# An attention walk over edges: one-hots written in 32 bits by VectorE without the widening copy, and a maximum moved ahead of collecting and one-hot

## The reference, cut to what matters

```
feat  = (h @ W).reshape(N, H, D)
e     = leaky_relu(el[src] + er[dst], 0.2)
emax  = segment_max(e, dst);  ex = exp(e - emax[dst])
denom = segment_sum(ex, dst)
rst   = segment_sum(feat[src] * (ex / denom[dst])[..., None], dst)
```

## Time and profile before

| | us |
|---|---|
| median of 3 runs | 6529.58 |
| lowest, highest | 6528.3, 12715.31 |
| profiled execution, its own time | 6532.67 |
| its span, first to last instruction | 6530.9 |

### The profile page before, as it was taken

The page is one execution under the profiler, slowest core; times in us unless marked ns, Lnnn a source line. Parts: engine busy times, 40 slices in busy tenths (PEclk is TensorE's granted clock), DMA queues, the critical chain, the costliest instruction groups (busy, mean ns, idle before and its releaser), DMA issues. The chain is left out here.

```text
span 6530.9 us, 127122 instructions
## 1 busy us (share of the span) xinstructions
PE 5098.4 (78%) x34156; PEld 4113.7 (63%) x34157; DVE 3381.7 (52%) x10342; ACT 2222.7 (34%) x6042; POOL 2219.6 (34%) x2057
## 2 busy tenths in 40 slices
PE   2665655428888888884797899999899997299997
PEld 1443332215555555554796688887788886299997
DVE  6898766528888888887455421113411114422222
ACT  0345666615555555556232300001200002433332
POOL 2577777765555555552221000000000000612221
PEclk8898777669999999995898999999999997599998
DMA  4478888875555555554565244442222223466665
GB/s 134 129 234 273 278 287 289 290 196 146 146 147 146 146 148 146 146 147 129 163 179 163 79 162 162 152 161 100 72 98 93 94 98 118 133 187 181 181 182 165
DMA packets 504762, 1057.75 MB, mean 162 GB/s; under 512 B 59670, under 2 KB 370317, under 8 KB 484972
## 3 DMA queue, kind: packets, MB, share of 16 engines
q1 hardware_dynamic: 385276, 706.86, 34.2%
q0 software_dynamic: 112144, 268.88, 15.0%
q10 hardware_dynamic: 7200, 80.28, 3.1%
HBM read 741.74 MB, written 323.21 MB: 163 GB/s over the span
## 5 line engine op out<-in xcount | busy, mean ns | idle before, releaser
L690 POOL DMA_INDIRECT arena<-table,arena x1664 | 1738.4, 1045 | 980.3 <-DVE arena L795 584.7
L1303 PE MATMUL banks<-arena 128*128 128x256 bf16 x14700 | 1623.7, 273 | 24.7 <-DMA arena<-counts 24.7
L1303 PEld LDWEIGHTS banks<-arena 128*128 128x128 f16 x14700 | 1439.5, 98 | 205.0 <-DMA arena<-counts 25.5
L869 PE MATMUL banks<-arena 128*128 128x261 f32 x3328 | 1009.5, 428 | 192.2 <-DVE arena L807 125.1
L620 PE MATMUL banks<-arena 128*128 128x392 bf16 x2368 | 602.2, 408 | 414.2 <-ACT banks L648 226.5
L2026 POOL DMA_INDIRECT expert_in<-arena,slot x147 | 161.2, 1097 | 2158.1 <-DVEq L1971 2116.4
L869 PEld LDWEIGHTS banks<-arena 128*128 128x128 f32 x3328 | 596.7, 199 | 330.5 <-DVE arena L807 134.0
L620 PEld LDWEIGHTS banks<-arena 128*128 128x128 bf16 x2368 | 338.2, 149 | 677.7 <-issue 635.4
L1357 DVE TENSOR_TENSOR rings<-rings,banks 128x256 f32<-128x256 f32 x98 | 41.3, 422 | 1344.1 <-PE banks L1295 1344.1
L2209 ACT ACTIVATE rings<-banks,b_sb 128x128 f32<-128x128 f32 x1296 | 370.5, 369 | 828.3 <-PE banks L2242 828.3
L795 DVE TENSOR_TENSOR arena<-arena 128x512 f32<-128x512 f32 x832 | 575.3, 692 | 141.4 <-ACT arena L742 140.4
(11 more groups left out here) (344 smaller groups left out, 5444.0 us busy)
## 6 DMA issues: line engine op xcount, KB each, us to landing
arena<-counts SPq DMA_DIRECT2D x100, 1568.0 KB, 6.7
arena<-in_L_ffn_W SPq DMA_DIRECT2D x114, 1024.0 KB, 5.2
edge_rows<-arena SPq DMA_DIRECT2D x416, 264.0 KB, 3.3
arena<-edge_rows SPq DMA_DIRECT2D x416, 264.0 KB, 2.9
counts<-arena ACTq DMA_DIRECT2D x50, 1568.0 KB, 6.8
arena<-in_L_ffn_w SPq DMA_DIRECT2D x64, 1024.0 KB, 5.2
expert_in<-arena SPq DMA_DIRECT2D x25, 2028.0 KB
arena<-table,arena POOLq DMA_INDIRECT x1664, 3.9
```

Of the source, the lines that this page charges most:

```text
L690: pool.indirect_dma_start(out=got[:, u, j, :], out_offset=None, in_=table0, in_offset=bass.IndirectOffsetOnAxis(ap=src_sb[:, 2 * pair + j: ...
L869: last = pe.matmul(banks_a[u][:, 0:mw], onehot[:, u, j, :], msg[:, u % RB, j, 0:mw], start=(j == 0), stop=(j == 1))
L1303: last = pe.matmul(psum[u][:, 0:D], a_ring[:, u, a, :], parts[:, a, k, :], start=(a == 0 and k == 0), stop=(a == NT - 1 and k == 2))
```

## The change

The 16-bit ring, its 16-bit targets and lane numbers, and ScalarE's widening copy go. VectorE writes the one-hot straight into the 32-bit `onehot`, eight pairs ahead, from 32-bit lane numbers and 32-bit targets. TensorE's turn reads the upper halves of those 32-bit values as 16-bit numbers (every second value, as before). `make_onehot` no longer waits for semaphores, since the collect of the same place lies ahead of it on VectorE. In VectorE's body the maximum of n+2 now follows straight behind `score_left` of n+2, ahead of the collect of n, and the one-hot comes last.

```diff
-                        def widen(i, u):
-                            n = UN * i + u
-                            act.wait_ge(s_oh, n + 1)
-                            wait(act, s_a, n - UN + 1)
-                            act.copy(onehot[:, u, :, :], hot16[:, u % RB, :, :].rearrange("p n j -> p j n")).then_inc(s_up, 1)
...
-                                if u + RB < UN or not final(i):
-                                    widen(i + (u + RB) // UN, (u + RB) % UN)
...
                         def make_onehot(i, u):
-                            n = UN * i + u
-                            wait(dve, s_t, n - RB + 1)
-                            wait(dve, s_up, n - RB + 1)
-                            dve.tensor_tensor(hot16[:, u % RB, :, :], pair_lanes,
-                                              near16[:, bass.ds(2 * pair_of(i, u), 2)].unsqueeze(1).broadcast_to([P, P, 2]),
+                            c = 2 * pair_of(i, u)
+                            dve.tensor_tensor(onehot[:, u, :, :], iota_n[:, :].unsqueeze(1).broadcast_to([P, 2, P]),
+                                              dst_sb[:, bass.ds(c, 2)].unsqueeze(2).broadcast_to([P, 2, P]),
                                               ALU.is_equal).then_inc(s_oh, 1)
...
-                        for u in range(RB + 1):
+                        for u in range(UN):
                             make_onehot(0, u)
...
                                 if two:
                                     score_left(*two)
-                                collect(i, u, tile(u))
                                 if two:
                                     score_max(*two)
-                                if u + RB + 1 < UN or not final(i):
-                                    make_onehot(i + (u + RB + 1) // UN, (u + RB + 1) % UN)
+                                collect(i, u, tile(u))
+                                if not final(i):
+                                    make_onehot(i + 1, u)
...
-                                last = pe.matmul(banks_t[u][:, j * P:(j + 1) * P], hot16[:, u % RB, :, j], ident16[:, :],
+                                last = pe.matmul(banks_t[u][:, j * P:(j + 1) * P], onehot16[:, u, j, :, 1], ident16[:, :],
                                                  start=True, stop=True)
...
                             pe.wait_ge(s_m, n + 1)
-                            pe.wait_ge(s_up, n + 1)
```

More of the change, by code:

```diff
@@ L656, in attend @@
                 tag, gw, mw = "gat_walk", AW, MW
-                s_oh, s_t, s_ht, s_b, s_z, s_w, s_m, s_a, s_acc, s_c, s_one, s_low, s_up, s_near = (
-                    sem(tag + "_" + n) for n in ("oh", "t", "ht", "b", "z", "w", "m", "a", "acc", "c", "one", "low", "up", "near"))
+                s_oh, s_t, s_ht, s_b, s_z, s_w, s_m, s_a, s_acc, s_c, s_one, s_low = (
+                    sem(tag + "_" + n) for n in ("oh", "t", "ht", "b", "z", "w", "m", "a", "acc", "c", "one", "low"))
                 s_g = [sem(f"{tag}_g{u}") for u in range(UN)]
@@ L662, in attend @@
                 KROUNDS = NKEPT // UN
[L663 to L666, removed]
                 zt = small[:, :].rearrange("p (u j h) -> p u j h", u=RB, j=2)
@@ L744, in walk_act @@
                         for u in range(3):
-                            widen(0, u)
                             copy_onehot(0, u)
-                        widen(0, 3)
                         weights(0, 0)
@@ L809, in walk_dve @@
                         dve.memset(msg[:, :, :, GW:AW], 1.0).then_inc(s_one, 1)
-                        dve.tensor_scalar(near16, dst_sb, 16384.0, None, ALU.min).then_inc(s_near, 1)
-                        dve.tensor_copy(pair_lanes, iota_n[:, :].unsqueeze(2).broadcast_to([P, P, 2])).then_inc(s_near, 1)
-                        dve.wait_ge(s_near, 2)
-                        for u in range(RB + 1):
+                        for u in range(UN):
                             make_onehot(0, u)
```

## The result

The changed kernel takes **6642.25 us** (median of 4 runs, 6640.77 to 6645.38), the kernel before 6529.8 on the same chip: a ratio of **1.0173, interval 1.0155 to 1.0191**, 112 us slower. By the bound of 2% that is no change; it is a measured loss all the same. One of the four executions of the kernel before took 12715.31; without it its median is 6529.58, and the ratio is taken from the other three. The profiled execution took 6640.77, with a span of 6639.0 against 6530.9.

The account below looks back on a forecast made before the run. VectorE bounds a plain pair, with a 0.20 us wait through ScalarE. Bodies of 15.98 against 14.45, times 104, give plus 159; the clock minus 32: 6660 profiled, 6657 us as median, range 6560 to 6725.

Parts of the forecast that it names:

- Left to maximum: VectorE, start to start: maximum now reads what left is still writing, 0.21 us instead of 0.08, a cost of 0.13.
- Maximum to collect: VectorE: collect's semaphore and register work stand exposed behind the maximum's wait, 0.28 us instead of 0.08, a cost of 0.20.
- Rival 1: Collect's register work stays hidden, maximum to collect 0.08, pair 1.70: 6480 to 6520 us; chance 0.11.
- The one-hot: VectorE writing 256 results in 32 bits: 0.34 us instead of 0.20 in 16 bits, a cost of 0.14.
- Sum to messages: VectorE, sum to the messages: 0.12 us instead of 0.39, as the wait for ScalarE goes, a gain of 0.27.
- Turn: Loop turn, once in 8 pairs: collect's semaphore and register work join its chain, 2.60 us against 2.42.
- Pair: One plain pair on VectorE, messages to messages: 1.90 us against 1.70 to 1.71.
- The clock: Later collects mostly cover TensorE's low-clock stretches in the walk: minus 32 us, ends 0 and minus 34.
- The sum: Whole kernel: 6532.67 + 159 - 32 = 6660 us for a profiled execution, 6657 as median.
- rival 2: Neither wait, left to maximum nor maximum to collect, costs anything: pair 1.57, 6390 us, faster; chance 0.02.
- rival 4: In between: part of the register work covered, or one-hot cheaper than its neighbour: 6530 to 6625 us; chance 0.11.
- Rival 3: TensorE's low clock comes for half of all pairs, each 2.22 us: +133, about 6790; chance 0.09, most near 6720.

Follow-up runs that it names:

- order alone: Kernel before with only the new order (left, maximum, collect, one-hot), 16-bit one-hot and widening copy kept: +55 and +52 us against the kernel before.
- fixed place: Collect adds to one fixed place for 7 of 8 pairs, sums wrong: in the changed kernel -34 us, in the kernel before -7, both against the kernel before.
- one-hot between: Kernel before with its 16-bit one-hot moved between left and maximum, collect last: -119 and -121 us against the kernel before.

## Why the prediction was right

It said 6657 and the range 6560 to 6725; 6642 is 15 below. (By the profiled executions, which its sum goes by, it is 6660 against 6640.77, 19 below.) Step by step, predicted and measured:

- **Left to maximum**, 0.21: 0.20. The rivals that it costs nothing fall: it is 0.20 in the changed kernel, in the order alone and with the fixed place, and left to whatever follows it is 0.08 or 0.09 wherever another operation stands between. The Trainium skill, "VectorE: DVE Perf Modes", on the DRAIN, has the semaphore at no extra cost; the rows say 0.12.
- **Maximum to collect**, 0.28: 0.26 and 0.31. Its make-up, 0.08 + register work + 0.05, holds for two sizes of that work, 0.046 (0.18) and 0.12 to 0.19 (0.26 to 0.31); with none the 0.05 goes too (0.08). Rival 1 falls by the two kernels with the fixed place. The Trainium skill, "Perfetto Trace Analysis", on the lifecycle of a DVE / Act engine instruction, lets the sequencer fetch on behind a queued instruction; here it does so behind an instruction that runs, but not behind one that waits.
- **The one-hot**, 0.34: 0.34 (2003.18 to 2003.52), duration 0.419.
- **Sum to messages**, 0.12 without a wait: 0.11 to 0.12. The wait for ScalarE fell from 140 us to 1.1.
- **Turn**, 2.60: 2.63. **Pair**, 1.90: 1.85, 1.90 or 1.95, by the length of the register work.
- **The clock**, -32: the mean clock rose only from 0.96 to 0.97, but a low stretch costs collect 0.27 where it cost 0.96. Collects wait 11.7 us for TensorE, 32.4 before. The bodies give the size. In the kernel before, 44 bodies with a low stretch take 15.30 and the others 14.47, which is 36 us in all; in the changed kernel 34 take 16.03 and 69 take 15.89, which is 5. So the clock gave 31, for the reason that the prediction had.
- **The sum**: 159 - 32 = 127 for the walk, measured 113.9. The miss of 13 is one of size. The body was built as 15.98; without a low stretch it is 15.89 in the mean (15.88 from the messages at 2010.07 to those at 2025.95). It was built on 14.45 for the kernel before, which is 14.47 in the mean. So the plus of 1.53 is 1.42, and the 159 are 148. Those 11 of the 13 lie for the most part in the register work, which was taken alike for all pairs, where those with the shorter work take 1.85. Another 6 us lie outside the walk, 4.1 of it in its earlier start, which is no larger than the difference between runs: luck, and not part of the reckoning.

The rivals: rival 1 (6480 to 6520), rival 2 (6390) and rival 4 (up to 6625) did not come. Rival 3 did not come in the changed kernel. A weaker form of it came in the half of the change that keeps the old one-hot: there the mean clock is 0.90, a low stretch falls in nearly every body, and it costs some 30 us, not the rival's 133. The prediction took it as a matter of how long TensorE idles per pair, and gave no reason for such a case.

What the prediction did not say is that the change's two halves hang on each other. It listed the one-hot as a cost of 0.14 in every pair. That is true only because the order takes the wait for ScalarE away; in the old order the wider one-hot costs nothing and, without the widening copy, gains 32. The bodies divide the 27.5 by which its walk is shorter: without a low stretch they take 14.36 against 14.47, 12 us, of which the turn has 0.05 (2.37, from 3000.71 to 3003.08, against 2.42) and the pair behind it 0.07 (1.76 against 1.83, medians over the walk); the other 15 or so are fewer low stretches (mean clock 0.98). Why leaving out the copy does either was not tested.

## What to carry to other kernels

Between two engines that wait for each other in a circle, write the pair as a sum up to the hand-over plus the larger of the two ways behind it; an edit is worth only what it does to the larger way, and two edits on different ways do not add. Register arithmetic on VectorE's sequencer was free here behind an instruction that ran (taking it away gave 7 us, interval 0.9981 to 1.0001), and behind one that waited it cost its full time and about 0.05 more (0.20 a pair for 0.15 of work), so put it, or the waiting instruction, elsewhere: filling a wait for one's own last result with an operation that is needed anyway (here the 16-bit one-hot between left and maximum) was worth 120 us, some 30 of them by TensorE's clock, where the change lost 112.

## What the runs showed of the hardware that was not expected

- TensorE's low clock comes in the walk in stretches that are nearly all 3.4 us long, and how often depends on the order of VectorE's work. In the changed kernel each of 33 such stretches begins 0.5 to 0.8 us behind the first messages after a turn. The mean granted clock over the walk is 0.96 before, 0.97 in the changed kernel, 0.90 (on either chip 0.89 to 0.90) with the order alone, and 1.00 with the one-hot between:

```profile
1430.00:2800.00 1370.00, 1153.63 (x6414) 791.95 (x6412) 1245.25 (x4808) 787.54 (x3205) 758.19 (x801) 1.00 0.56 158
```

What decides it is not shown. Ahead of the low stretch of the order alone, TensorE had been idle 1.19 and then 0.52 ahead of its next additions. But an earlier body of the same run has 1.22 and 0.53, and there the granted clock stays at 1.00 (from 1450 to 1463). These are the rows of the one and of the other:

```profile
2002.06 1.14 PE L869 MATMUL banks<-arena 128*128 128x261 f32 x4 [1.19 <-DVE arena L807]
...
2003.87 2.10 PE L869 MATMUL banks<-arena 128*128 128x261 f32 x4 [0.52 <-DVE arena L795]
```

```profile
1451.81 1.14 PE L869 MATMUL banks<-arena 128*128 128x261 f32 x4 [1.22 <-DVE arena L807]
...
1453.64 1.14 PE L869 MATMUL banks<-arena 128*128 128x261 f32 x4 [0.53 <-DVE arena L795]
```

Nor does the changed kernel bear out a rule by these idle times: they are 1.14 and 0.78 at the stretch of 1516.84, and 1.13 and 0.81 in the body at 2008.78, where the clock stays up. What can be said is that two of the faster orders, the 16-bit one-hot between and the kernel before without ScalarE's first step, gained twice, once by the shorter pair and once, by some 30 us, by the clock.

- What a low stretch costs is another matter than how often it comes. With ScalarE's first step left out of the changed kernel the mean clock is 0.95 over the same 1500 us, lower than the changed kernel's 0.97, at the same time.
